# Masked keys of heads 4 to 7 by transfers between standing zeros, and the second pair of heads 0 to 3 on GpSimd

## The reference, cut to what matters

```python
q = (x @ Wq.T).reshape(B, S, NHEAD, hd).transpose(0, 2, 1, 3)      # first attention, window of 64
k = (x @ Wk.T).reshape(B, S, NHEAD, hd).transpose(0, 2, 1, 3)
scores = einsum('bhnqd,bhnkd->bhnqk', qb, k2) / sqrt(D)             # masked, softmax, times v

k = einsum('ihd,bpd->biph', W_K, x); q = einsum('ihd,bpd->biph', W_Q, x)
scores = einsum('biph,biqh->biqp', k, q)                            # second attention, causal
```

## Time and profile before

| | |
|---|---|
| median of three runs | 236.61 us (236.32 to 239.23) |
| profiled execution: span from first to last instruction | 235.1 us |
| granted TensorE clock over the span | 1.000 |
| busy PE, DVE, ACT, POOL | 224.4, 205.3, 168.2, 91.5 us |
| chain that ended last | PE 62%, DVE 20%, POOL 9%, ACT 3%, DMA 2% |

### The profile page before, as it was taken

How to read it: one execution, slowest core, us unless ns; L and a number is a source line. 1 busy time by engine, 2 the same in 40 slices (tenths; PEclk the granted TensorE clock), 3 DMA queues, 4 the chain that set the end, 5 groups by cost and what they waited for, 6 DMA issues and landing times.

```text
span 235.1 us, 4622 instructions
## 1 busy us (share of the span) xinstructions
PE 224.4 (95%) x1493; PEld 172.6 (73%) x1494; DVE 205.3 (87%) x524; ACT 168.2 (72%) x498; POOL 91.5 (39%) x155
## 2 busy tenths in 40 slices
PE   7899898799999999998999999999999999999995
PEld 2597576567776678675876677888888888888885
DVE  3778888986998989999899878999999995999886
ACT  2367355699869987899869999567649766666660
POOL 6200315648895867276734849932000000000000
PEclk9999999999999999999999999999999999999999
DMA  6910000000320200030000114411110004412001
GB/s 193 369 38 4 0 0 0 1 3 0 97 86 6 89 0 3 0 88 6 3 1 0 64 39 136 128 45 47 46 45 0 3 0 138 133 60 78 0 1 45
DMA packets 9464, 11.71 MB, mean 50 GB/s; under 512 B 721, under 2 KB 6097, under 8 KB 9313
## 3 DMA queue, kind: packets, MB, share of 16 engines
q1 hardware_dynamic: 9008, 11.16, 15.3%
q10 hardware_dynamic: 432, 0.27, 0.4%
HBM read 10.87 MB, written 0.56 MB: 49 GB/s over the span
## 4 chain that ended last, share of the span: by engine, by line
PE 62%; DVE 20%; POOL 9%; ACT 3%; issue 2%; DMA 2%; SPq 0%; POOLq 0%; ACTq 0%; DVEq 0%
PE bank L1047 6%; PE bank L1050 6%; PE bank L1035 6%; PE bank L1048 6%; PE bank L1037 6%; PE bank L1036 6%; DVE negmax L1478 6%; PE bank L959 4%; POOL w_lo L434 3%; PE bank L935 3%; PE bank L893 2%; PE bank L984 2%; DVE ht L1440 2%; POOL w_hi L432 2%; DMA xs<-x 2%
## 5 line engine op out<-in xcount | busy, mean ns | idle before, releaser
L618 ACT ACTIVATE hb<-bank,pk 128x512 f32<-128x512 f32 x64 | 43.0, 701 | 21.0 <-PE bank L1037 20.8
L1528 DVE TENSOR_TENSOR hlo<-hb,hhi 128x512 fp32r<-128x512 f32 x64 | 45.1, 727 | 3.1 <-ACT hhi L621 2.0
L588 ACT ACTIVATE prob<-bank,negmax 128x192 f32<-128x192 f32 (+1 forms) x64 | 28.7, 480 | 5.3 <-DVE negmax L1478 5.2
L1478 DVE TENSOR_REDUCE negmax<-bank 128x2 f32<-128x384 f32 (+2 forms) x48 | 29.6, 640 | 2.8 <-PE bank L941 2.5
L434 POOL TENSOR_TENSOR w_lo<-w_raw,w_hi 128x256 fp32r<-128x256 f32 x32 | 25.2, 788 | 2.6
L1047 PE MATMUL bank<-hhi,w_hi 128*128 128x512 f32 (+2 forms) x68 | 25.9, 381 | 0.0
L1050 PE MATMUL bank<-hlo,w_hi 128*128 128x512 f32 (+2 forms) x68 | 25.8, 379 | 0.0
L1048 PE MATMUL bank<-hhi,w_lo 128*128 128x512 f32 (+2 forms) x68 | 25.8, 379 | 0.0
L1035 PE MATMUL bank<-xhi,w_hi 128*128 128x512 f32 x64 | 25.4, 396 | 0.0
L544 ACT ACTIVATE probT<-bank 128x512 f32<-128x512 f32 x38 | 22.7, 627 | 3.4 <-PE bank L959 1.8
L1037 PE MATMUL bank<-xhi,w_lo 128*128 128x512 f32 x64 | 25.0, 390 | 0.0
(11 more groups left out here) (159 smaller groups left out, 524.3 us busy)
## 6 DMA issues: line engine op xcount, KB each, us to landing
w_raw<-w SPq DMA_DIRECT2D x16, 256.0 KB, 3.1
comb_b<-routes SPq DMA_DIRECT2D x16, 256.0 KB, 3.2
pk<-packed SPq DMA_DIRECT2D x1, 1280.0 KB, 8.8
pk<-packed SPq DMA_DIRECT2D x1, 560.0 KB, 6.1
xs<-x SPq DMA_DIRECT2D x3, 128.0 KB, 2.6
out<-acc SPq DMA_DIRECT2D x3, 128.0 KB, 1.7
xs<-x ACTq DMA_DIRECT2D x1, 128.0 KB, 2.8
pk<-packed ACTq DMA_DIRECT2D x1, 68.0 KB, 2.6
```

The source lines that it names most:

```text
L588: last = nc.scalar.activation(prob_of(n, u)[:, of], lane[n][u % 2][:, of], ACT.Exp, bias=negmax[n][:, unit_query(u), h:h + 1], accum_out=s ...
L618: nc.scalar.activation(hb[blk % 2][:, j, :], h_bank[j][:, :], ACT.Relu, bias=bias).then_inc(h_ready, 1)
L1478: V.tensor_reduce(negmax[n][:, unit_query(u), heads[0]:heads[-1] + 1], lane[n][u % 2][:, :].rearrange("q (h k) -> q h k", h=len(heads))[:, ...
L1528: V.tensor_tensor(hlo[blk % 2][:, j, :], hb[blk % 2][:, j, :], hhi[blk % 2][:, j, :].bitcast(F32), ALU.subtract).then_inc(hlo_ready, 1)
```

## The change

- Heads 4 to 7 are no longer computed. GpSimd sets these four heads of `kM` to zero once for each lane (`zero_keys`: lane 1 at the start, lane 0, whose memory belongs to the first attention's q and k until then, after the last score of that attention). In every pass SyncE then copies the 16 rows of each head, upper and lower half apart, from `k_parts` to their places in `kM` (`place_keys`): eight transfers of 16 rows of 1 KB for each image, 64 in all. Unit 3 waits until all eight of its image have landed.
- SyncE's list is now a braid of `load_next_weights` and `place_keys`.
- The second pair of heads 0 to 3 of every image moves to GpSimd (`masked_keys` there: two instructions in place of four), with a semaphore of its own, `kM_more_ready`, for unit 1. VectorE and ScalarE make the first pair only.
- On GpSimd `masked_keys(0, 2)` and `masked_keys(0, 3)` move ahead of `split_weights(2, 0)` and `(2, 1)`.

```diff
+            def load_next_weights(e):
+                sp.wait_ge(w_ready, PIECES * (e - 1))
+                load_weights(e)
+
+            def place_keys(a, n):
+                l = n % 2
+                sp.wait_ge(kM_zeroed[l], 1)
+                sp.wait_ge(k_parts_ready[l], passed(a, n) + 1)
+                for h in range(HG, HEADS):
+                    for half in range(2):
+                        rows = slice(64 * half + HD * (h % HG), 64 * half + HD * (h % HG) + HD)
+                        sp.dma_start(kM[l][rows, h, :].bitcast(F32), k_parts[l][rows, h // HG, :].bitcast(F32)
+                                     ).then_inc(kM2_ready[l], 16)
...
-            for e in range(2, E):
-                sp.wait_ge(w_ready, PIECES * (e - 1))
-                load_weights(e)
+            place_keys(0, 1)
+            place_keys(0, 0)
+            load_next_weights(2)
+            place_keys(0, 2)
+            place_keys(0, 3)
+            load_next_weights(3)
+            load_next_weights(4)
+            place_keys(1, 1)
+            place_keys(1, 0)
+            load_next_weights(5)
+            place_keys(1, 3)
+            place_keys(1, 2)
+            load_next_weights(6)
+            load_next_weights(7)
...
+            def zero_keys(l):                                  # GpSimd
+                if l == 0:
+                    pool.wait_ge(s0_full, B)
+                G.memset(kM[l][:, HG:HEADS, :].bitcast(F32), 0.0).then_inc(kM_zeroed[l], 1)
+            zero_keys(1)
...
             def masked_keys(a, n):                             # GpSimd
                 pool.wait_ge(k_parts_ready[n % 2], passed(a, n) + 1)
-                for h in range(HG, HEADS):
-                    last = G.tensor_scalar(kM[n % 2][:, h, :], k_parts[n % 2][:, h // HG, :].bitcast(F32),
+                for h in unit_heads(n, 2):
+                    last = G.tensor_scalar(kM[n % 2][:, h, :], k_parts[n % 2][:, 0, :].bitcast(F32),
                                            const("headmask", h, h + 1), 1.0, ALU.mult, ALU.mult)
-                last.then_inc(kM2_ready[n % 2], 1)
+                last.then_inc(kM_more_ready[n % 2], 1)
...
+                if j == 1:                                     # GpSimd, before the second group norm's power
+                    zero_keys(0)
...
             split_weights(1, 3)
+            masked_keys(0, 2)
+            masked_keys(0, 3)
             split_weights(2, 0)
             split_weights(2, 1)
-            masked_keys(0, 2)
-            masked_keys(0, 3)
             power(1, 1)
...
-            masked_keys(0, 1, 0)                               # ScalarE; likewise for (0, 3), (1, 1), (1, 3)
+            masked_keys(0, 1)
             upper_queries(0, 1)
-            masked_keys(0, 1, 1)
...
-                if u in (0, 1):                                # TensorE, scores
-                    pe.wait_ge(kM_ready[n % 2], 2 * passed(a, n) + u + 1)
+                if u == 0:
+                    pe.wait_ge(kM_ready[n % 2], passed(a, n) + 1)
+                if u == 1:
+                    pe.wait_ge(kM_more_ready[n % 2], passed(a, n) + 1)
                 if u == SECOND_HALF:
-                    pe.wait_ge(kM2_ready[n % 2], passed(a, n) + 1)
+                    pe.wait_ge(kM2_ready[n % 2], 2 * HG * 16 * (passed(a, n) + 1))
...
-            masked_keys(0, 0, 0)                               # VectorE; likewise for (0, 2), (1, 0), (1, 2)
+            masked_keys(0, 0)
...
-            masked_keys(0, 0, 1)
```

More of the change, by code:

```diff
@@ L213, in build @@
                 "ak_full", "aq_full", "k_hi_ready", "q_hi_ready", "k_parts_ready", "q_lo_ready", "atv_full"))
-        kM_ready, kM2_ready, av_ready = (sems(n, LANES) for n in ("kM_ready", "kM2_ready", "av_ready"))
+        kM_ready, kM_more_ready, kM2_ready, av_ready = (
+            sems(n, LANES) for n in ("kM_ready", "kM_more_ready", "kM2_ready", "av_ready"))
+        kM_zeroed = sems("kM_zeroed", LANES)
         mixed, rb_ready, rT_full, rT_ready, attn_ready, wo_full, t_ready = (
@@ L567, in upper_queries, with masked_keys @@
                      ).then_inc(q_hi_ready[n % 2], 1)
-            def masked_keys(a, n, pair):
+            def masked_keys(a, n):
                 act.wait_ge(k_parts_ready[n % 2], passed(a, n) + 1)
-                for h in unit_heads(n, 2 * pair):
+                for h in unit_heads(n, 0):
                     last = copy(kM[n % 2][:, h, :], k_parts[n % 2][:, 0, :].bitcast(F32),
@@ L728, in _ @@
             inverse_sums_turned(0, 0)
-            masked_keys(0, 3, 0)
+            masked_keys(0, 3)
             inverse_sums_turned(0, 1)
-            masked_keys(0, 3, 1)
             exps(0, 2, 0)
@@ L758, in _ @@
             probs_turned(0, 2, 5)
-            masked_keys(1, 1, 0)
+            masked_keys(1, 1)
             probs_turned(0, 3, 5)
@@ L764, in _ @@
             inverse_sums_turned(0, 3)
-            masked_keys(1, 1, 1)
             exps(1, 0, 0)
@@ L793, in _ @@
             probs_turned(1, 0, 5)
-            masked_keys(1, 3, 0)
+            masked_keys(1, 3)
             upper_queries(1, 2)
@@ L798, in _ @@
             upper_queries(1, 3)
-            masked_keys(1, 3, 1)
             exps(1, 2, 0)
@@ L1456, in lower_queries, with masked_keys @@
                                        ).then_inc(q_lo_ready[n % 2], 1)
-            def masked_keys(a, n, pair):
+            def masked_keys(a, n):
                 dve.wait_ge(k_parts_ready[n % 2], passed(a, n) + 1)
-                first = unit_heads(n, 2 * pair)[0]
+                first = unit_heads(n, 0)[0]
                 heads = slice(first, first + 2)
@@ L1745, in _ @@
             inverse_sums(0, 1)
-            masked_keys(0, 2, 0)
+            masked_keys(0, 2)
             lower_keys(0, 3)
             copy_values(0, 2)
-            masked_keys(0, 2, 1)
             normalize(0, 0)
@@ L1784, in _ @@
             lower_keys(1, 0)
-            masked_keys(1, 0, 0)
+            masked_keys(1, 0)
             copy_values(1, 1)
-            masked_keys(1, 0, 1)
             lower_queries(1, 0)
@@ L1824, in _ @@
             lower_keys(1, 2)
-            masked_keys(1, 2, 0)
+            masked_keys(1, 2)
             copy_values(1, 3)
-            masked_keys(1, 2, 1)
             lower_queries(1, 2)
```

## The result

The changed kernel takes 248.44 us (median of 4 runs, 245.28 to 251.92) beside 236.64 us for the kernel before (4 runs): a ratio of 1.0448, 95% interval 1.0394 to 1.0501. It is slower by 4.5%, and the forecast was 236.0 us. One of the four, 251.92 us, is a slow execution, which the ratio leaves out; the other three took 245.28 to 248.88 us. The profiled execution after took 248.88 us with a span of 247.0 us, 11.9 us more than before.

The account below looks back on a forecast made before the run. No engine alone was taken to bound the passes: TensorE full, VectorE and ScalarE nearly so, handing work to each other. Gains of 0.28 + 0.25 + 0.1 = 0.63 us from 236.61 gave 236.0 us, range 235.3 to 237 (chance 0.62).

Parts of the forecast that it names:

- the price of an issue: On SP's queue, each transfer was taken to issue 0.47 us after the last, ends 0.35 and 0.74.
- X: Time from the first image's keys being ready until the second image's transfers have landed, predicted at 8.6 us.
- the prediction's own comparison: Waits at unit 3: X less 9.25, 10.1, 12.5 and 9.4 us available in passes 1 to 4; none expected.
- The transfers come late: Rival: SP's 16 serial issues cost more than 0.47 us each; 245 us at 0.74, over 239 us, chance 0.08.
- point of decision: At X = 11.4, or 0.66 us an issue, the waits at unit 3 pass 5.4 us, 2% of the kernel and the gain.
- the 0.74 row: A weight load whose issue took 0.74 us, explained by a full queue and a preceding transfer of many small pieces.
- The landing: Issue to landing of a transfer, taken as 1.53 us, upper end 3.64; about 2.0 by the skill page.
- The gains: Savings of 0.28 us in pass 1, 0.25 in pass 2 and 0.1 in pass 3, none in pass 4: 0.63 us.
- The 0.25 of pass 2: Fewer GpSimd copies end the norm's 0.49 us wait for `power(1, 1)`; 0.25 us comes through, ends 0 and 0.49.
- the 0.6 to 0.9 that were named as a sign: VectorE's idle time ahead of the first `largest` of passes 3 and 4 rises by 0.6 to 0.9 us.
- VectorE as the bound: Rival: the removed work on the chain all comes off, 234.6 or 233.2 us; range 231.5 to 235.3, chance 0.15.
- The zeros: GpSimd's two memsets of about 1.0 us each cost nothing, covered by idle time; without cover 1 us each.

Follow-up runs that it names:

- two_queues: The changed kernel with the 64 transfers issued by two engines, SP for images 1 and 3 and GpSimd for images 0 and 2: 238.34 us, ratio 1.0044.
- asked_first: The changed kernel with image 2's transfers issued ahead of image 3's in pass 4, the order in which TensorE asks: 246.21 us, ratio 1.0339.
- no_transfers: The changed kernel without transfers and zeros, GpSimd multiplying the second pair and heads 4 to 7 of every image: 237.64 us, ratio 1.0036.

## Why the prediction was wrong

**The step that failed is the price of an issue: "Size matters little, so I take 0.47".** The first half held. But every row behind the 0.47 had an end in HBM, and these transfers have none; there the same SP needs 0.63 us. With the landing of 1.8 us in place of 1.53, X is 15 x 0.63 + 1.8 = 11.3 us instead of 8.6, and the stretched issues bring it to 11.9 to 12.7. Put into the prediction's own comparison, 11.9 - 9.25, 12.6 - 10.1 and 12.7 - 9.4 give 2.7 + 2.5 + 3.3 = 8.5 us of waiting; the traces show 8.9. One of the prediction's own signs of being wrong, issues above 0.6 us, came true.

**The rival was there, and priced nearly right.** "The transfers come late" gave 245 us at 0.74 us an issue, and with the clock held up the kernel takes 244.01. Its point of decision, X = 11.4, was passed. But an issue costs 0.63; only with the stretched ones is the mean of a block 0.67 to 0.72 us, and no row was read for that, so the closeness of 245 is partly luck. The rival had 0.08 because the 0.74 row was explained away and 0.47 came from six rows; but six rows of another kind of transfer are one observation. The explanations were wrong, too: no row shows a full queue at 77.36, where a single load had been issued just before, and the load of that row is itself the one of many small pieces. What the trace really told was a wider span: SP's timeline before also has issues of 1.30 us (at 4.05) and 1.56 us (at 132.31), which the prediction did not use. It named 0.74 as an end, and then its range left it out. The Trainium skill's rule against transfers under 64 KB (page "DMA: Bandwidth & Descriptors", rules for kernel authors), which was cited for this rival, agrees with these runs: 64 transfers of 16 KB cost 40 us of SP's issuing at 0.63 us each.

**The landing** was 1.7 to 3.3 us, median 1.8, within the bounds. Alone it would have cost pass 1 nothing: 15 x 0.47 + 1.8 = 8.9 us is still under 9.25. (With 2.0 us, which the prediction tried as well, its 9.05 us would give pass 1 a wait of 0.1 us once the pass had gained 0.28, not the 0.4 that it says.)

**The clock** was in no term. The waits themselves were priced; that what follows a wait may run at 1.2 GHz was not, and it cost 3.9 us, a third of the loss.

**The gains** were right in sum, 0.62 us measured without the transfers against 0.63, but by luck, since their places were not. Pass 1 gave 0.39, not 0.28: TensorE's scores, too, had waited for the removed instruction, which no step counted (TensorE's timeline before):

```profile
45.45 0.50 PE L935 MATMUL bank<-kM,q_hi 128*128 128x512 f32 x1 [0.15 <-DVE kM L1464]
```

The 0.25 of pass 2 appeared (0.35) and was mostly gone by pass 3. Pass 3 gave nothing, not 0.1: of the removed 0.83 us 0.60 came back as VectorE's waits, the least of the 0.6 to 0.9 that were named as a sign, though for ScalarE's `q_hi` and not for TensorE; in pass 4 it was 0.52. Pass 4 gave 0.18, not nothing. VectorE as the bound is refuted: with its four instructions gone and no transfers in the way, the passes shrink by 0.6 us, not by 2 to 3.

**The zeros** were right: 0.95 us each for an estimate of 1.0, under the same cover. SP's later weight load, moved behind the transfers, left no wait that the traces show.

**What stays open.** Each block has one issue stretched to 1.1 to 1.8 us, and beside it an instruction fetch of 16 KB stands in the trace, here in the window from 49.9 to 50.0 us (queue, packets, MB, share):

```profile
q8 instruction: 1, 0.02, 62.8%
```

The issue that begins at 50.05 is the stretched one. This holds in all eleven traces: behind the start's first 6.2 us SP has 31 issues of over 0.8 us, and every one overlaps a fetch on q8. The two blocks of sixteen into which no fetch falls, pass 4 with the clock kept up and pass 2 of the run with the other order, have no issue over 0.60 us. Transfers with an end in HBM are stretched as well, and the trace before had one, beside a fetch that begins at 132.22 (SP's timeline before):

```profile
132.31 1.56 SPq L336 DMA_DIRECT2D w_raw<-w  x1
```

So fetch and stretched issue go together wherever they were seen; that the one makes the other was not tried. Nor do the runs tell why the clock stayed up behind the 2.91 us wait of pass 2: the length of a wait does not tell it alone, since it fell behind one of 1.86 us.

## What to carry to other kernels

Price a transfer by a row of the same kind, both of its ends in the same memories; if the trace has none, the ends of the range are the forecast, and a series of n issues multiplies the doubt by n. Compare n times the spacing plus one landing with the time to the first consumer, and set the margin beside that doubt: here 0.7 us of margin stood against 15 x (0.74 - 0.47) = 4 us. Look for the longest issue in the timeline, too, not only for the common one. Where TensorE is left waiting for some microseconds, count the time after the wait as well.

## What the runs showed of the hardware

- An issue on SP with both ends in SBUF came 0.62 to 0.68 us after the last, with 8, 16, 32 or 128 rows; with one end in HBM 0.44 to 0.47, stretched issues aside. GpSimd issued the same SBUF transfers 0.49 us apart (8 in 3.92 us).
- 16 KB inside SBUF landed 1.8 us after its issue (median of 64), and 1.7 us when GpSimd issued it (median of 32).
- TensorE's clock fell to the 1.2 GHz level behind waits of 1.86, 2.12 and 2.87 us and during waits of 2.85 and 3.39 us; it stayed up through waits of 1.59, 1.68 and 2.91 us (two_queues 1.86; asked_first 2.12, 2.85, 1.68; no_transfers 1.59; the changed kernel the others). With twelve matmuls on idle data (eleven in the trace, 2.54 us) ahead of the three waits it stayed at 1.0.
- All 31 issues of SP that lasted over 0.8 us behind the start overlap a 16 KB instruction fetch (eleven traces).
